# Edge counts of a graph network gathered in windows of 32 destinations, with a folded source key and early composed tiles

## The reference

```python
# layer A: messages, sums, a GRU cell, a batch norm with given statistics
m   = relu(concat([x[src], edge_attr]) @ W1.T + b1) @ W2.T + b2
agg = segment_sum(m, dst)
h   = gru(agg, x);  x = layernorm(x + x + batchnorm(h))
# layer B, twice (relu between): w[r] = sum_b att[r, b] * basis[b], 30 bases of 512x512
msg = sigmoid(x[dst] @ gate_w[r]) * x[dst] @ w[r]          # r: the edge's type
out = segment_sum(msg, src) + x @ root + bias
x   = layernorm(x + out)
```

## Time and profile before

| | us |
|---|---|
| timed runs, median of 3 | 600.06 (598.46 to 602.71) |
| the profiled execution | 594.98 |
| its span, first to last instruction | 593.2 |
| TensorE busy | 549.6 (93%) |
| VectorE busy | 298.1 (50%) |
| ScalarE busy | 136.0 (23%) |
| GpSimd busy | 118.4 (20%) |

### The profile page before, as it was taken

One profiled execution on the slowest core, in us unless ns is written; L12 is line 12 of the kernel. 1 busy time (PEld: TensorE's weight loads), 2 busy tenths in 40 slices (PEclk: granted clock), 3 DMA queues, 4 the chain that ended last, 5 costly groups with the idle time before them and its releaser, 6 DMA issues.

```text
span 593.2 us, 7336 instructions
## 1 busy us (share of the span) xinstructions
PE 549.6 (93%) x2229; PEld 288.7 (49%) x2230; DVE 298.1 (50%) x634; ACT 136.0 (23%) x211; POOL 118.4 (20%) x148
## 2 busy tenths in 40 slices
PE   0999999889988988899999999989999999999996
PEld 0343443444444444454333333323455665887774
DVE  4777797878797878204041424223462312234233
ACT  0011101433343433306121121211232201033100
POOL 0000051457665751000000000800200003800000
PEclk9999999999999999899999999999999999999999
DMA  7930061568866763596888888897979885910000
GB/s 206 393 138 0 36 177 39 180 209 248 263 207 205 247 210 107 215 429 224 317 312 309 312 308 308 306 352 238 363 258 418 324 328 177 227 71 2 19 36 36
DMA packets 30673, 129.80 MB, mean 219 GB/s; under 512 B 4707, under 2 KB 8627, under 8 KB 25909
## 3 DMA queue, kind: packets, MB, share of 16 engines
q1 hardware_dynamic: 18980, 99.53, 44.6%
q0 software_dynamic: 11520, 29.37, 18.0%
q10 hardware_dynamic: 144, 0.52, 0.2%
HBM read 118.40 MB, written 11.01 MB: 218 GB/s over the span
## 4 chain that ended last, share of the span: by engine, by line
PE 78%; DMA 13%; DVE 3%; issue 3%; DVEq 1%; SPq 1%; ACT 1%
PE ps L1088 14%; PE ps L1033 11%; DMA basis<-in_basis 11%; PE ps L940 9%; PE ps L955 8%; PE ps L992 8%; PE ps L1127 6%; PE ps L967 5%; PE ps L968 4%; PE ps L1071 3%; PE ps L919 3%; PE ps L909 2%; DVE rlo L732 2%; DMA xT<-in_xT 1%; PE ps L1068 1%
## 5 line engine op out<-in xcount | busy, mean ns | idle before, releaser
L955 PE MATMUL ps<-X 128*128 128x512 f32 x160 | 73.7, 602 | 0.0
L524 ACT ACTIVATE rhi<-x 128x512 fp32r<-128x512 f32 x80 | 49.0, 631 | 82.5 <-DVE x L725 81.1
L470 POOL DMA_INDIRECT X<-u_rows,esrc x40 | 42.8, 1069 | 119.7 <-DMA u_rows<-X 75.0
L992 PE MATMUL ps<-basis,sel 128*32 128x512 f32 x512 | 59.3, 596 | 5.9 <-DMA basis<-in_basis 4.9
L479 POOL DMA_DIRECT2D w_hi<-w_layer x32 | 16.9, 673 | 219.7 <-DMA w_layer<-ev 219.7
L702 DVE TENSOR_SCALAR X<-iota,keyf 128x1280 bf16<-128x1280 f16 x96 | 52.7, 549 | 13.1 <-PE ps L940 10.4
L940 PE MATMUL ps<-X 128*128 128x512 bf16 (+1 forms) x288 | 57.3, 345 | 0.1
L1088 PE MATMUL ps<-X,R 128*128 128x512 f32 x120 | 55.5, 605 | 0.0
L1088 PE MATMUL ps<-X,xT 128*128 128x512 f32 x120 | 54.5, 596 | 0.0
L732 DVE SCALAR_TENSOR_TENSOR rlo<-x,rhi 128x512 fp32r<-128x512 f32 x80 | 51.5, 686 | 0.1
L967 PE MATMUL ps<-rhi,oh 128*128 128x512 f32 x96 | 40.1, 417 | 11.1 <-DVE rlo L732 7.1
(11 more groups left out here) (167 smaller groups left out, 664.9 us busy)
## 6 DMA issues: line engine op xcount, KB each, us to landing
basis<-in_basis SPq DMA_DIRECT2D x30, 2048.0 KB, 11.4
w_layer<-ev SPq DMA_DIRECT2D x15, 512.0 KB, 12.4
X<-in_eaT SPq DMA_DIRECT2D x20, 256.0 KB, 2.9
basis<-in_basis SPq DMA_DIRECT2D x8, 512.0 KB, 6.3
w_hi<-w_layer POOLq DMA_DIRECT2D x32, 128.0 KB, 3.7
w_lo<-w_layer POOLq DMA_DIRECT2D x32, 128.0 KB, 4.5
X<-in_WihT SPq DMA_DIRECT2D x1, 3072.0 KB, 11.3
X<-in_WhhT SPq DMA_DIRECT2D x1, 3072.0 KB, 18.2
```

The costliest lines, as they stand in the source:

```text
L470: nc.gpsimd.indirect_dma_start(gat[e % GATHERS], None, t["u"][:, :], bass.IndirectOffsetOnAxis(ap=esrc[:, e:e + 1], axis=0)).then_inc(gat_ ...
L524: nc.scalar.activation(rhi[:, h, s], pre[:, s], ACT.Relu).then_inc(hi_ready, 1)
L955: pe.matmul(ps[:, EA_BANKS[s]], eaT[:, h % 2, s * P:(s + 1) * P], W1bT, start=True, stop=True).then_inc(ea_done, 1)
L992: mm = pe.matmul(bank[32 * g:32 * g + 32], sel[:, layer, s], basis[:, c % SLOTS, g, s2], start=(s == 0), stop=(s == 3), tile_position=(0, ...
```

## The change

- **Windows of 32.** Counts are gathered for 20 windows of 32 destinations, not 5 of 128, over edge tiles in pairs, not fours. Loop bounds are made on 20 partitions at once, with two small products with the identity, and loaded per window (`window_span`).
- **Folded key.** The 1280 source columns are folded to 320 (SPAN): the quarter of the column (type, and whether src is 320 or more) moves into the destination one-hot, whose 128 columns are 4 quarters x 32 destinations (`pattern`, `codef`). One matmul of 320 columns takes the place of three. The one-hots lie in a ring of 8 slots. ScalarE copies each window out in 4 pieces of 32 x 320, each with its own sum.
- **Interleaved work.** Only source rows 0 stand ahead of the counts; the other four are done in halves after windows 0 to 7. Three composed tiles, not one, are made in halves after windows 8, 9, 13, 14, 18 and 19, with drains further on; the job list holds 12 composed tiles in place of 14, besides the first.
- **Two queues.** W1aT and xT are issued from ScalarE's queue, the rest from SyncE's, in another order: batch-norm rows and W2T behind the source rows' stores, basis tiles 2 to 5 behind them.
- **Moved.** The bias casts and the 16 small products that fill `sel` go from VectorE to ScalarE; the edge loop's bounds are made behind the counts.

The core of the diff (the removed loops are those printed above; the steps that make the bounds and keys are left out):

```diff
-EARLY_BANK = 3
+EARLY = 3
+WIN = 32
+WINS = NP // WIN
+FOLD = P // WIN
+SPAN = REL * NP // FOLD
+PAIR = 2
+PAIRS = ET // PAIR
+RING = 8
+EARLY_AT = (8, 13, 18)
...
-    composed.pop(0)
+    for _ in range(EARLY):
+        composed.pop(0)
...
+        hot = X[:, 9216:9216 + RING * (P + SPAN) // 2].bitcast(BF16).rearrange("p (s n) -> p s n", s=RING)
+        pattern = X[:, 14160:14224].bitcast(F16)
+        codef = X[:, 14224:14304]
...
-            if c >= 2 * SLOTS:
+            if c >= SLOTS:
                 old = c - SLOTS
-                if old % 2:
+                if old % 2 and old < 2 * EARLY:
+                    eng.wait_ge(early_full, old // 2 + 1)
...
+        def window_span(eng, w):
+            v = eng.value_load(gspan[0:1, 2, w:w + 1], min_val=0, max_val=GPACK * GPACK * (WINS + 2) * PAIRS)
+            first = (v % GPACK).with_bounds(min_val=0, max_val=PAIRS - 1)
+            end = (v // GPACK % GPACK).with_bounds(min_val=1, max_val=PAIRS)
...
+            ranks = t["tab"][:, 1, 0, 0:WINS].rearrange("o t -> t o")
+            for a, b in ((drow[:], t["dstrow"]), (ident[:], t["ident"]), (win, ranks)):
                 sp.dma_start(a, b).then_inc(span_in, 16)
-            for a, b in ((esrc, t["src"]), (edst, t["dst"]), (etyp, t["typ"]), (iota, t["iota"])):
+            for a, b in ((iota, t["iota"]), (esrc, t["src"]), (edst, t["dst"]), (etyp, t["typ"])):
...
+            for c in range(SLOTS):
+                load_basis(sp, c)
+            sp.dma_start(W1bT, t["W1bT"]).then_inc(w1b_in, 16)
...
+            for i, a in enumerate(t["bn"]):
+                sp.dma_start(bn_rows[:, i], a.broadcast_to([P, H])).then_inc(const_in, 16)
+            sp.dma_start(W2T[:], t["W2T"]).then_inc(w2_in, 16)
+            for c in range(SLOTS, SLOTS * EARLY):
+                load_basis(sp, c)
...
+            act.dma_start(W1aT, t["W1aT"]).then_inc(w1a_in, 16)
+            for n in range(NT):
+                act.dma_start(xT[:, :, n * P:(n + 1) * P], t["xT"][:, :, n * P:(n + 1) * P]
+                              ).then_inc(xt_in[n], 16)
+            act.wait_ge(bias_in, 48)
+            nc.scalar.copy(picks[:], picks_raw)
+            nc.scalar.copy(bias[:], bias_raw).then_inc(bias_parts, 1)
...
+            act.wait_ge(att_ready, 1)
...
+            last.then_inc(sel_ready, 1)
             drain_u(0)
-            drain_u(1)
-            for j in range(NT):
...
+            for w in range(WINS):
+                act.wait_ge(ct_acc, w + 1)
+                for q in range(FOLD):
+                    at = slice(WIN * (w % FOLD), WIN * (w % FOLD + 1))
+                    nc.scalar.activation(CT[at, w // FOLD, q * SPAN:(q + 1) * SPAN],
+                                         ps[WIN * q:WIN * (q + 1), w % 3, 0:SPAN], ACT.Copy,
+                                         accum_out=part_cnt[at, w // FOLD, q:q + 1]).then_inc(ct_drained, 1)
+                if w % 2 and w // 2 + 1 < NT:
+                    drain_u(w // 2 + 1)
+                for i in range(EARLY):
+                    if w == EARLY_AT[i] + 1:
+                        act.wait_ge(early_full, i + 1)
+                        nc.scalar.copy(early_ev[i][:, 0], ps[:, 3 + i % 2]).then_inc(upper_ready, 1)
+                    if w == min(EARLY_AT[i] + 4, WINS - 1):
+                        act.wait_ge(early_drained, i + 1)
+                        act.dma_start(t["w"][0][i], early_ev[i][:].bitcast(F32)).then_inc(w_out, 16)
...
+            dve.wait_ge(spans_in_sbuf, 1)
+            ahead = window_span(dve, 0)
...
+            def drain_early(i):
+                dve.wait_ge(upper_ready, i + 1)
+                dve.tensor_tensor(early_ev[i][:, 1], ps[:, 3 + i % 2], early_ev[i][:, 0].bitcast(F32), ALU.subtract
+                                  ).then_inc(early_drained, 1)
+            for w in range(WINS):
+                (first, end, before), ahead = ahead, window_span(dve, (w + 1) % WINS)
+                with dve.Fori(first, end) as g:
+                    at = (g + before) % (RING // PAIR)
+                    for s in range(PAIR):
+                        dve.wait_ge(hot_free, (g + before) * PAIR + s + 1)
+                        one = hot[:, bass.ds(at * PAIR + s, 1)].rearrange("p s n -> p (s n)")
+                        dve.tensor_scalar(one[:, 0:P], pattern, float(WIN * w), codef[:, bass.ds(g * PAIR + s, 1)],
+                                          ALU.add, ALU.is_equal)
+                        dve.tensor_scalar(one[:, P:P + SPAN], iota[:, 0:SPAN], keyf[:, bass.ds(g * PAIR + s, 1)],
+                                          None, ALU.is_equal).then_inc(hot_ready, 1)
+                if w == 0:
+                    dve.wait_ge(span_row, 1)
+                    dve.tensor_reduce(maskc[:], ident[:].rearrange("p (b c) -> p c b", c=BLK), AX.X, ALU.add)
+                    dve.tensor_copy(sprow[:, 0:2], ps[0:1, 4, 0:2 * ET].rearrange("p (q t) -> p q t", q=2))
+                    step(dve.tensor_copy(att[:].rearrange("p g l r -> p (g l r)"), ps[:, 4, 256:256 + 4 * REL]))
+                    dve.memset(att[0:(2 * GROUP - BASES) * BLK, 1], 0.0).then_inc(att_ready, 1)
+                for i in range(EARLY):
+                    if w == EARLY_AT[i] + 4:
+                        drain_early(i)
...
+            dve.wait_ge(ct_drained, FOLD * WINS)
+            dve.tensor_reduce(cnt[:], part_cnt, AX.X, ALU.add).then_inc(cnt_ready, 1)
...
+            def source_rows(n, half):
                 bank = ps[:, 6 + n % 2]
-                for k in range(KT):
+                if half == 0:
+                    pe.wait_ge(w1a_in, 16)
+                    pe.wait_ge(xt_in[n], 16)
+                    if n >= 2:
+                        pe.wait_ge(u_drained, n - 1)
+                for k in (2 * half, 2 * half + 1):
                     pe.matmul(bank, xT[:, k, n * P:(n + 1) * P], W1aT[:, k], start=(k == 0), stop=False)
+                if half == 1:
+                    if n == 0:
+                        pe.wait_ge(bias_ready, 1)
+                    add_bias(bank, 1, 0, 2, start=False).then_inc(u_acc, 1)
...
+            def compose_early(i, group):
+                if group == 0:
+                    pe.wait_ge(sel_ready, 1)
+                    if i >= 2:
+                        pe.wait_ge(early_drained, i - 1)
+                mm = compose(ps[:, 3 + i % 2], 0, i, (group,))
+                if group == 1:
+                    mm.then_inc(early_full, 1)
+            source_rows(0, 0)
+            source_rows(0, 1)
+            pe.wait_ge(spans_in_sbuf, 1)
+            ahead = window_span(pe, 0)
+            for w in range(WINS):
+                if w >= 3:
+                    pe.wait_ge(ct_drained, FOLD * (w - 2))
+                bank = ps[:, w % 3, 0:SPAN]
+                pe.matmul(bank, zer[:, 0:P], zer[:, 0:SPAN], start=True, stop=True)
+                (first, end, before), ahead = ahead, window_span(pe, (w + 1) % WINS)
+                with pe.Fori(first, end) as g:
+                    at = (g + before) % (RING // PAIR)
+                    for s in range(PAIR):
+                        pe.wait_ge(hot_ready, (g + before) * PAIR + s + 1)
+                        one = hot[:, bass.ds(at * PAIR + s, 1)].rearrange("p s n -> p (s n)")
+                        pe.matmul(bank, one[:, 0:P], one[:, P:P + SPAN], start=False, stop=True,
+                                  skip_group_check=True).then_inc(hot_free, 1)
+                pe.matmul(bank[:, 0:64], zer[:, 0:P], zer[:, 0:64], start=False, stop=True,
+                          skip_group_check=True).then_inc(ct_acc, 1)
+                if w // 2 + 1 < NT:
+                    source_rows(w // 2 + 1, w % 2)
+                for i in range(EARLY):
+                    if w in (EARLY_AT[i], EARLY_AT[i] + 1):
+                        compose_early(i, w - EARLY_AT[i])
...
+            pe.wait_ge(ct_drained, FOLD * WINS)
+            pe.wait_ge(early_drained, EARLY)
+            pe.wait_ge(wins_ready, 1)
```

More of the change, by code:

```diff
@@ L63 @@
 PACK = 8
-GPACK = 32
+GPACK = 64
 BN_EPS = 1e-5
@@ new lines, in compose @@
+            def compose(bank, layer, tile, groups=(0, 1)):
+                for group in groups:
+                    c = 2 * (layer * WT + tile) + group
+                    pe.wait_ge(basis_in[c % SLOTS], 16 * (c // SLOTS + 1 + 3 * (c >= SLOTS * EARLY)))
+                    for s2 in range(2):
+                        s = 2 * group + s2
+                        for g in range(4):
+                            mm = pe.matmul(bank[32 * g:32 * g + 32], sel[:, layer, s],
+                                           basis[:, c % SLOTS, g, s2], start=(s == 0), stop=(s == 3),
+                                           tile_position=(0, 32 * g))
+                    if group == 0:
+                        mm.then_inc(basis_used, 1)
+                return mm
```

250 lines of the change are left out of this document (102 added, 148 removed).

## The result

The changed kernel takes **628.72 us**, median of four runs (625.97 to 630.96), against 600.20 (598.46 to 602.71) of the kernel before on the same chip: a ratio of 1.048, 95% interval 1.044 to 1.052. It is 4.8% slower, where I had forecast 572 us and a range of 556 to 590. Its profiled execution took 630.25 us with a span of 628.3, against 593.2 before.

The account below looks back on a forecast made before the run. TensorE was taken to bound the kernel from 240.3 us on, with TensorE and VectorE both near their limit in counting. Terms -9.3 - 7.5 - 2 - 9 = -27.8 us took the median 600.06 to 572 us, range 556 to 590.

Parts of the forecast that it names:

- Start of counting, -9.3: Before the first counts: earlier weight loads and less work ahead let counting start near 16.2 us, not 25.50; -9.3 us.
- loads no earlier: Rival at the start: basis tiles beside W1aT delay its landing, counting starts at 21, 577 us; chance 0.1.
- The count loop, -7.5: Counting stage: VectorE's instruction stream may bind, 64 us for 118 tiles in 20 windows against 71.5; -7.5 us.
- two one-hots a tile make 0.32: Counting stage: a tile's share of VectorE's instruction stream, taken as two one-hots at 0.16 us each.
- The 0.16 us: Edge loop trace: from a matmul's end at 130.03 to its released one-hot at 130.19, used as price per one-hot.
- the stream is the bound: Rival in the 20 counting windows: VectorE's or TensorE's stream takes 0.63 us a tile, 100 us, 608 total; chance 0.08.
- From counting to the edge loop, -2: Stretch between last count and edge loop: about 6 us instead of 8.15; -2 us.
- Two composed tiles fewer late, -9.0: Late job list: its last two composed tiles disappear, 3.9 + 5.1 us; -9.0 us, other end -5.
- At nothing: Parts priced at no change: count reduction, attribute loads, W2T and batch-norm rows, and gathers, which start earlier.
- Signs given ahead: Trace signs: ScalarE drains 0.4 us with 0.19 behind, no compose after first output product, 344 us after the edge loop.
- I am wrong if tiles stand 0.5 us apart: Counting stage: stated sign of failure; tiles themselves 0.5 us apart would mean no gain.

Follow-up runs that it names:

- the loop of fours: Changed kernel with tiles gathered by fours in four fixed slots, not by pairs in a ring of 8, making 156 tiles instead of 118: 618.7 us.

## Why the prediction was wrong, step by step

**Start of counting, -9.3:** partly. TensorE's first counting matmul moved by 4.2 us (25.5 to 21.33), VectorE's first one-hot by 6.6, and VectorE's counts, since its stream sets the stage. The rival "loads no earlier" (counting at 21) was nearest. I had counted how early the weights are issued and not what they do to the loads beside them. The rule of the Trainium skill, "DMA: Bandwidth & Descriptors", section "Issuing engines are not separate DMA queues", was quoted for the weights' landing; the runs agree that the engines are shared, but what it cost shows in the 40 KB loads, 5.7 us for 1.8, while W1aT itself landed 5.0 us after its issue (6.9 before).

**The count loop, -7.5: the step that failed**, by its term "two one-hots a tile make 0.32", 118 x 0.32 + 20 x 1.27. Measured, a tile's share is 0.835 us and a window's change 0.73: 118 x 0.835 + 20 x 0.73 = 113 us. The 0.16 us was the way from a matmul's end to a one-hot that had stood waiting for it, idle for 2.61 us; what the instructions ahead of it cost does not show in that step. The window I had too dear, by 0.5 us.

A nearer estimate was within reach. The kernel before takes 0.63 us a tile with 22 instructions for four tiles, so its stream needs at most 2.5 us for them, 0.114 each. A pair has 14: 1.59 us at that price, 0.80 a tile. It is no bound, for instructions differ in price, and the pair measured 1.67. I took the 0.63 over unchanged for the rival, though half as many tiles share a branch and each carries more address arithmetic. The mechanism was the rival "the stream is the bound", with a chance of 0.08 and a price of 608; at 0.80 a tile and 1.27 a window, 119 us and the one for window 0, it would have read 628.

**Branches, in no term:** the Trainium skill, "Advanced Engine Details and Errata", section "Control Flow Timing", gives some 108 ns for a compare-and-branch. No run isolates one, and what is left for it by subtraction differs. The step over the pair loop's end is 0.98 us with four register instructions and the branch, where three without a branch take 0.35 in all; at 0.10 us each the branch is left with some 0.5. The step over the end of the loop of fours is 0.75 us, with six register instructions (14 besides the eight one-hots, less seven inside and the branch) and the branch, and by the same price next to nothing is left. So whether the page's figure holds here stays open.

**From counting to the edge loop, -2:** 1.5, right.

**Two composed tiles fewer late, -9.0:** 6.4 by the timed run (3 to 10), 5.5 in the profile. The tiles went; the waits did not:

```profile
414.31 1.92 PE L1013 MATMUL ps<-basis,sel 128*32 128x512 f32 x16
419.08 3.59 PE L1013 MATMUL ps<-basis,sel 128*32 128x512 f32 x16 [2.85 <-DMA basis<-in_basis]
```

A wait of 2.85 us where the earlier trace rows had a longest of 2.2, and behind it half a tile at 3.59 us, not 1.92: TensorE had stood idle and went on at the lower clock (granted 0.52 in these 3.59 us, 1.00 before the wait and after them). I priced what is removed and let everything else stand. That is worth some 2 us of the 3.5 missing; the rest may be scatter, for a second profile of the same kernel, with the same wait (3.21) and slow half (3.53), has 344.2 us for the late phase, 8.7 less than before.

**At nothing:** the edge loop took 2.0 us more in this trace. It took 136.8 us in the second profile of the same kernel, and 135.3 to 135.9, as before, in eleven of the thirteen variants that also have three early tiles (137.9 and 140.3 in the other two). So the early tiles alone do not make it longer; I have no cause for that.

**Signs given ahead:** drains of 0.43 and 0.19 us as said (L557), no compose after the first output product, 347 us for the late phase (344 said). "I am wrong if tiles stand 0.5 us apart" was the sentence that held: they stand 0.52 and 1.15 apart.

## What to carry to other kernels

Price a loop by its instructions per turn, register and branch ones included, from the built program; an estimate of each comes from the tightest loop in the trace, even where it hides behind work (here 5% too low, 1.59 us for 1.67). An engine's idle time is not slack of its instruction stream: before shrinking the work of a turn, see that the turn is still longer than its stream, on every engine that runs it. A bulk load moved earlier, though it goes to another queue, can delay the small loads that a chain of dependent steps begins with; put those first and the bulk right behind, on one queue.

## What I had not expected of the hardware

- A load of 40 KB took 1.8 us from issue to landing, and 5.7 to 5.9 us beside W1aT and xT on another engine's queue. Five issues of 256 KB took 16.0 us of ScalarE's time when another queue's 4 MB were issued as they began (4.84 us when they went first), and ScalarE did nothing else meanwhile.
- A no-op with a semaphore increment costs VectorE's stream 0.10 us; a loop turn of 14 instructions 1.67 us, one of 22 with simpler addresses 2.03.
- In the thinned-out counting the granted clock fell from 1.00 to 0.76 on the mean, and in some stretches to the lower level of 1.2 GHz:

```profile
90.00:100.00 10.00, 5.26 (x15) 1.31 (x14) 5.45 (x21) 4.38 (x16) 0.00 (x0) 0.50 0.48 198
```

TensorE had waited some 0.75 us ahead of every pair. It cost little, as VectorE's stream was longer, but half a composed tile behind such waits (at 131.37) took 3.64 us, not 1.92.
